# A sixteen-pair software pipeline on one core: the rounding number moves from VectorE to ScalarE, and every engine's loop gets another order

## What is computed

```python
x = _layernorm(x + _L0_attn_ref(x, ...))            # 512 -> 64 channels, 4 layers of decaying scan + MLP, -> 512
x = _layernorm(x + _L0_xattn_ref(x, ctx, ctx))      # autocorrelation attention
x = _layernorm(x + _L0_ffn_ref(x, weight, bias))    # x and weight rounded to MXFP4, one 512x512 product
```

## Time and profile before

| | us |
|---|---|
| median of 3 runs | 321.08 (320.82 to 321.69) |
| profiled execution, its own time | 323.65 |
| its span (first to last instruction) | 321.6 |
| first stage, span 0 to about 126 | 126 |
| pair loop, `attended(0)` to the end | 195 |
| one iteration in the middle of the loop | 9.95 |

### The profile page before, as it was taken

The page is one execution under the profiler, slowest core; times in us unless marked ns, Lnnn a source line. Parts: engine busy times, 40 slices in busy tenths (PEclk is TensorE's granted clock), DMA queues, the critical chain, the costliest instruction groups (busy, mean ns, idle before and its releaser), DMA issues.

```text
span 321.6 us, 4437 instructions
## 1 busy us (share of the span) xinstructions
PE 274.6 (85%) x1060; PEld 109.8 (34%) x1060; DVE 269.8 (84%) x871; ACT 231.1 (72%) x541; POOL 174.7 (54%) x226
## 2 busy tenths in 40 slices
PE   1597988989889887888998999999998888977762
PEld 1223222322222222254433554434444244422220
DVE  5969989889888894358999999999999989869580
ACT  6046789899799797967666687778877776745534
POOL 1026513204204014023378888999999999997842
PEclk9999899999999999999999999999999999979987
DMA  6999999602113200600000000111101102011122
GB/s 207 396 273 354 325 160 213 128 23 65 36 33 85 78 0 17 116 1 2 2 0 16 17 14 6 50 49 18 51 34 51 51 16 51 34 50 49 51 82 99
DMA packets 22576, 26.54 MB, mean 83 GB/s; under 512 B 10771, under 2 KB 11411, under 8 KB 22550
## 3 DMA queue, kind: packets, MB, share of 16 engines
q1 hardware_dynamic: 20470, 22.06, 21.9%
q0 software_dynamic: 2080, 4.19, 7.7%
HBM read 15.89 MB, written 4.19 MB: 62 GB/s over the span
## 4 chain that ended last, share of the span: by engine, by line
DVE 30%; ACT 20%; PE 18%; issue 15%; POOL 11%; DMA 3%; SPq 1%; POOLq 0%; DVEq 0%; ACTq 0%
DVE big L1172 5%; DVE m L1153 4%; DVE X L1107 3%; DVE big L1142 3%; DMA big<-in_xT_dram 3%; PE ps L380 3%; ACT big L654 3%; DVE ps L1203 3%; ACT L752 2%; DVE ps L1081 2%; ACT X L682 2%; PE ps L562 2%; POOL big L925 2%; POOL big L931 2%; DVE big L1277 2%
## 5 line engine op out<-in xcount | busy, mean ns | idle before, releaser
L654 ACT ACTIVATE big<-X,lnv 128x512 f32<-128x512 f32 x48 | 34.2, 713 | 15.0 <-DVE X L1107 15.0
L1107 DVE SCALAR_TENSOR_TENSOR X<-ps,X 128x512 f32<-128x512 f32 x48 | 32.1, 682 | 10.7 <-PE ps L415 6.1
L391 PE MATMUL ps<-ctx_ring,consts 64*128 64x512 f32 (+1 forms) x96 | 35.8, 643 | 0.0
L441 PEld LDWEIGHTS ps<-consts,big 96*128 96x128 f32 x256 | 29.8, 191 | 13.4 <-issue 10.6
L441 PE MATMUL ps<-consts,big 96*128 96x64 f32 x256 | 32.0, 278 | 1.1 <-DVE big L1142 1.1
L1184 DVE TENSOR_TENSOR big<-ps,ctxf 128x512 f32<-128x512 f32 x48 | 30.8, 683 | 2.0 <-PE ps L475 1.3
L682 ACT ACTIVATE X<-X,lnv 128x512 f32<-128x512 f32 x32 | 25.8, 808 | 0.6
L1172 DVE MATCH_REPLACE8 big<-w,big 128x64 f32<-128x64 f32 x128 | 25.1, 210 | 0.0
L838 POOL TENSOR_TENSOR big<-big 128x512 f32<-128x512 f32 x4 | 5.8, 1444 | 35.5 <-DVE big L1250 25.5
L918 POOL TENSOR_TENSOR big<-big 128x512 f32<-128x512 f32 x15 | 19.0, 1268 | 6.2 <-DVE big L1172 6.0
L1142 DVE TENSOR_TENSOR big<-ps,ctxf 96x512 f32<-96x512 f32 x32 | 20.4, 677 | 0.8 <-PE ps L428 0.8
(11 more groups left out here) (188 smaller groups left out, 675.9 us busy)
## 6 DMA issues: line engine op xcount, KB each, us to landing
big<-in_xT_dram SPq DMA_DIRECT2D x4, 1024.0 KB, 9.4
ctx_ring<-in_ctx_dram SPq DMA_DIRECT2D x16, 256.0 KB, 4.0
out_dram<-X SPq DMA_DIRECT2D x16, 256.0 KB, 2.0
X<-in_x_dram SPq DMA_DIRECT2D x2, 1536.0 KB, 11.4
X<-rows_sb POOLq DMA_DIRECT2D x1, 3072.0 KB, 21.6
X<-in_wq_dram SPq DMA_DIRECT2D x1, 1024.0 KB, 5.6
X<-in_x_dram SPq DMA_DIRECT2D x2, 512.0 KB, 3.9
X<-rows_sb POOLq DMA_DIRECT2D x1, 1024.0 KB, 8.0
```

What stands on the lines that cost most here:

```text
L391: mm(bank(LANE_BANK[lane]), mat((CY_0, CY_1, CY_C)[f])[half, :], ctx_ring[half, r * N:(r + 1) * N], start=True, stop=True).then_inc(s_cfor ...
L441: last = mm(ps[:, 2 * N + j * P + b * L:2 * N + j * P + (b + 1) * L], PQ[0:EVEN, b * N + j * P:b * N + (j + 1) * P], mat(IC_E)[0:EVEN, 0:L ...
L654: squared[k, n] = chain(a(JUNK[k], row(n), ACT.Square, bias=st[:, 0:1], scale=-float(V), accum_out=st[:, 2:3]))
L1107: stt(row(m), bank(b), 0.0, row(m), ALU.add, ALU.add, accum_out=st[:, 0:1]).then_inc(s_sum[k], 1)
```

## The change

On VectorE `rounding` becomes `exponents`: the mask alone. The number is made by a new ScalarE step `rounding_numbers`, one ACTIVATE (Copy) with scale and bias from bank 1 into `MB`: `SLOPE * e + FLOOR` lies in the same power of two as `max(e, 0.25) * MAGIC` for each e that can occur, so that it rounds alike. A semaphore `s_expo` passes from VectorE to ScalarE and to GpSimd's clamp. The loops of all five engines get another order and other distances; some one-time work (the last weight transposes, now into bank 7, and the last layernorm of the first stage) moves with them. `kept_busy` now stands at two places with 10 and 12 products; before 24 at six.

```diff
-DRAIN_BUSY = ((0, 4), (6, 6), (5, 3))
+DRAIN_BUSY = {LAST + 6: 10, LAST + 7: 12}
+SLOPE, FLOOR = 3.25 * 2.0 ** 20, 1.125 * 2.0 ** 20
...
             # sync
-            for n in range(PAIRS + 3):
+            for n in range(PAIRS + 5):
                 quantized_to_channels(n)
-                stored(n - 3)
+                stored(n - 5)
...
             # tensor
-            for t in range(1, PAIRS + 11):
-                weights_to_time(t - 7)
-                out_even(t - 8)
-                weight_rest_forms(t - 7)
-                weight_forms(t - 7)
-                correlation(t - 5)
...
-                query_forms(t - 4)
-                feed_forward(t - 10)
...
-                quantized_to_channels(t - 9)
-                out_rest(t - 7)
-                projection(t)
+            for t in range(1, PAIRS + 9):
+                weight_rest_forms(t - 5)
...
+                weight_forms(t - 5)
+                correlation(t - 3)
...
+                projection(t)
+                quantized_to_channels(t - 8)
+                feed_forward(t - 8)
+                query_forms(t - 2)
+                if t in DRAIN_BUSY:
+                    pe.wait_ge(s_sum[0], PAIRS)
+                    kept_busy(DRAIN_BUSY[t])
+                out_rest(t - 5)
+                weights_to_time(t - 4)
+                out_even(t - 5)
...
             # scalar
+            def rounding_numbers(n):
+                if here(n) and n < LAST:
+                    act.wait_ge(s_expo, n + 1)
+                    a(MB, bank(1), ACT.Copy, bias=FLOOR, scale=SLOPE).then_inc(s_magic[1], 1)
...
             # gpsimd, clamped
+                    pool.wait_ge(s_expo, n + 1)
+                    chain.then_wait(g_.tensor_scalar(VB, VB, 1.5, -1.5, ALU.min, ALU.max))
                     pool.wait_ge(s_magic[1], n + 1)
-                    chain.then_wait(g_.tensor_scalar(VB, VB, 1.5, -1.5, ALU.min, ALU.max))
...
             # vector
-                    do(ts(bank(1).bitcast(I32), VB.bitcast(I32), 0x7F800000, None, ALU.bitwise_and))
-                    ts(MB, bank(1), 0.25, MAGIC, ALU.max, ALU.mult).then_inc(s_magic[1], 1)
+                    ts(bank(1).bitcast(I32), VB.bitcast(I32), 0x7F800000, None, ALU.bitwise_and).then_inc(s_expo, 1)
```

More of the change, by code:

```diff
@@ L463, in weight_rest_forms @@
                     if n == 0:
-                        pe.wait_ge(s_act, 4 * SLOTS)
+                        pe.wait_ge(s_qe[0], VC)
                     if n >= 1:
@@ L602, in _ @@
                 slot(m)
[L603 to L618 removed]
+            for t in range(1, PAIRS + 9):
+                weight_rest_forms(t - 5)
+                if t == 4:
                     pe.wait_ge(s_sq1, SLOTS + 2)
                     mm(bank(4), mat(MEAN), SQ_LAST, start=True, stop=True).then_inc(s_var1, 1)
[L621 to L625 removed]
+                weight_forms(t - 5)
+                correlation(t - 3)
                 if t == 2:
                     mixed(SLOTS)
+                    transposes(0, VC, bank(7), XQ[0])
+                projection(t)
[8 more added lines that the diff above has]
+                out_even(t - 5)
         @block.scalar
@@ L779, in _ @@
             for t in range(PAIRS + 10):
-                squares(0, t)
-                corr_out(t - 3)
+                log_sum(t - 3)
+                squares(2, t - 9)
+                weights_out(t - 4)
+                rounding_numbers(t - 6)
                 if t == 3:
-                    weight_channels(VC - 1)
-                squares(2, t - 9)
-                if t == 2:
-                    act.wait_ge(s_mlp, SLOTS)
-                    a(SQ_LAST, XC[1], ACT.Square, bias=base[:, DEPTH:DEPTH + 1]).then_inc(s_sq1, 1)
-                quantized_out(t - 7)
-                factors(0, t - 1)
-                top_exponentials(t - 3)
-                weights_out(t - 4)
-                log_sum(t - 3)
-                normalise(0, t - 1)
-                last_factors(t - 9)
-                squares(1, t - 5)
-                factors(1, t - 5)
-                normalise(1, t - 5)
-                if t == 4:
                     act.wait_ge(s_var1, SLOTS + 2)
@@ L802, in _ @@
                 probabilities(t - 3)
+                squares(1, t - 5)
+                factors(1, t - 5)
+                normalise(1, t - 5)
+                squares(0, t)
+                corr_out(t - 2)
+                factors(0, t)
+                normalise(0, t)
+                top_exponentials(t - 2)
+                last_factors(t - 9)
+                if t == 0:
+                    act.wait_ge(s_mlp, SLOTS)
+                    a(SQ_LAST, XC[1], ACT.Square, bias=base[:, DEPTH:DEPTH + 1]).then_inc(s_sq1, 1)
+                if t == 1:
+                    weight_channels(VC - 1)
+                quantized_out(t - 8)
         @block.gpsimd
@@ L950, in block_scaled @@
                     scaled(1, row(n), n % 2, n + 1)
-            for t in range(PAIRS + 8):
-                block_scaled(t - 3)
+            for t in range(PAIRS + 9):
+                finished(t - 9)
+                rounded_off(t - 4, clamped(t - 4))
                 chosen(t - 1)
                 top_differences(t)
-                finished(t - 7)
-                mark = clamped(t - 3)
+                block_scaled(t - 3)
                 differences(t)
-                rounded_off(t - 3, mark)
         @block.vector
@@ L1193, in block_scales, with exponents @@
                     scales(1, row(n), n % 2, bank(4)[:, 0:NBLK])
-            def rounding(n):
+            def exponents(n):
                 if here(n) and n < LAST:
@@ L1285, in _ @@
                 slot(m)
-            for t in range(PAIRS + 9):
+            for t in range(PAIRS + 7):
+                top_sum(t - 3)
                 attended(t)
-                weight_products(t - 6)
-                block_scales(t - 7)
-                without_largest(t - 5)
-                last_chosen(t - 5)
-                fed(t - 9)
-                last_quantized(t - 7)
-                largest(t - 4)
-                if t == 6:
+                exponents(t - 6)
+                last_quantized(t - 6)
+                query_products(t - 2)
+                crossed(t - 5)
+                without_largest(t - 3)
+                last_chosen(t - 3)
+                weight_products(t - 4)
+                block_scales(t - 5)
+                largest(t - 2)
+                if t == 5:
                     last_norm(1, RS_LAST)
-                rounding(t - 7)
-                top_sum(t - 4)
-                query_products(t - 3)
-                crossed(t - 6)
+                fed(t - 7)
 def kernel(**inputs):
```

16 lines of the change are left out of this document (3 added, 13 removed).

## The result

| | before | changed |
|---|---|---|
| median | 322.27 (20 runs, 320.49 to 324.73) | **324.25** (20 runs, 322.67 to 330.71) |
| ratio, 95% interval | | **1.0059** (1.003 to 1.0087) |
| mean granted clock of an execution | 0.973 to 0.996 (runs of before beside the experiments) | 0.960 to 0.976 (one 0.949) |

The account below looks back on a forecast made before the run. It took a ring through ScalarE's layernorm and VectorE, closed once per 9.95 iteration, as the bound; GpSimd's 9.66 came next. Pairs 3 to 15 -4.0 and drain -1.0 gave -5.0: 316.1, range 312.5 to 320.4.

Parts of the forecast that it names:

- The middle: Pairs 3 to 15 by top_sum: 119.2 before, 115.2 after, from two iterations of 9.3 and ten of 9.66; -4.0.
- two places of 0.2: In TensorE's 9.79 iteration, L475 and L441 start later than the column stream needs; so 9.4 at least, 9.6 taken.
- the first window: One pair-loop iteration before the change, 232.03 to 241.98; attended was said to have run out ten iterations later.
- the hand-off: From MAX8's end through GpSimd and ScalarE to top_sum's start: 0.78, read from pair 0.
- VectorE's ring: VectorE's iteration, head to MAX8's end 8.41, plus hand-offs of 0.78 through GpSimd and ScalarE to top_sum: 9.2 together.
- its wait at the head: At the head of VectorE's iteration: a wait of some 0.5 for ScalarE's L699, a sign the forecast is right.
- The slower rival: ScalarE's waits stay and it becomes the bound: 10.3 an iteration, 324.3 in all; chance 0.12.
- The rival that TensorE holds: The iteration stays 9.95 because TensorE's 9.79 is real; only the drain gains: 320.1; chance 0.11.
- I leave pair 3 at 165.49: Ramp: pair 0 comes about 0.7 earlier, ScalarE's waiting order gives it back by pair 3; bounds -0.9 and +0.9.
- The drain: From top_sum to fed of pair 15: 31.1 before, 30.1 after; -1.0, bounds -2.5 and +1.2.
- The sum: Whole kernel: -4.0 for pairs 3 to 15 and -1.0 at the end make -5.0; span 316.6, forecast 316.1.
- the sign to look for: Sign of a wrong forecast: over 32 from last top_sum to last residual sum, TensorE's granted clock falling earlier than before.

Follow-up runs that it names:

- again: The changed kernel run and profiled once more, nothing altered: 325.6 (7 runs), ratio 1.0077 against the kernel before.
- warm: Changed kernel plus 16 idle TensorE products in the ramp's waits (iterations 2 and 4): 324.18 (12 runs), ratio 1.0004.
- drain_sbuf: Changed kernel with the block maxima of the last three pairs alone in SBUF, not bank 4: 322.91 (12 runs), ratio 1.0001.
- scales_sbuf: Changed kernel with the block maxima of the pairs in SBUF, not bank 4: 324.7 (12 runs), ratio 1.0075.
- no_holes: Changed kernel with drain_sbuf's edit, warm's idle products, 6 more in iteration 3, 14 behind the last out_even, 5 for 12 before the last transposes: 321.2, ratio 0.9978.

## Why the prediction was wrong

- **The middle**, pairs 3 to 15, forecast -4.0: measured -4.3. The mean iteration was right, its reason was not. I made GpSimd the bound at 9.66 and gave TensorE 9.6; TensorE's own round is 9.78, GpSimd's 9.49. The step that failed is the sentence on "two places of 0.2" inside TensorE's 9.79, which I took to be slack for the new order. They are no slack: from L467 to L475 and to L441 it takes 1.06 and 1.08 in before, and from L468 to L476 and to L442 1.06 and 1.06 in again (rows below). What the new neighbours cost (L487 to L456 takes 0.97 where L486 to L415 took 0.86, and L527 to L429 0.97 where L526 to L486 took 0.87), others gave back (L442 to L416 takes 1.83 where L441 to L428 took 1.92). That the total fits is luck: the twelve iterations aren't alike, four of 9.08 to 9.68 come first, then five of 9.78, then 9.64 and two of 9.47, 9.58 on average against the forecast's 9.60. Timelines of TensorE, before and again:

```profile
235.35 1.12 PE L467 MATMUL ps<-big,consts 128*128 128x512 f32 x2
236.41 1.15 PE L475 MATMUL ps<-big,consts 64*128 64x512 f32 x4
237.49 2.00 PE L441 MATMUL ps<-consts,big 96*128 96x64 f32 x16
```
```profile
238.52 1.13 PE L468 MATMUL ps<-big,consts 128*128 128x512 f32 x2
239.58 1.13 PE L476 MATMUL ps<-big,consts 64*128 64x512 f32 x4
240.64 2.00 PE L442 MATMUL ps<-consts,big 96*128 96x64 f32 x16
```

- **Smaller misreadings.** `attended` has run out two iterations after the first window, not ten. For pair 0 MAX8 ends at 140.87 (139.76 + 1.11), not 140.79, so the hand-off is 0.70 and VectorE's ring 9.1. Neither moves the sum.
- **VectorE and ScalarE.** VectorE is busy 9.23 of an iteration (forecast 9.02), and its wait at the head, 0.21, is for TensorE's L527 and not 0.5 for L699. The copy L684 takes 0.59 (forecast 0.60), and GpSimd waited for it 0.19 once in the middle. The slower rival, ScalarE's waits surviving, didn't come: ScalarE is busy 8.67 of 9.77. That its time, 324.3, is almost the measured 324.25 is chance: the iteration is not 10.3, and the loss lies at the ends. The rival that TensorE holds was right on the engine and wrong on the time.
- **The ramp**, "I leave pair 3 at 165.49": +2.8 from the first `attended`. This step failed. I followed who normalises first, and never asked what TensorE does between the last slot and the pair loop when its work comes earlier than its inputs. 2.4 of it goes with the clock (warm), 0.4 with the order itself.
- **The drain**, forecast -1.0, bound +1.2: +3.3. This step failed too. The sum followed GpSimd's and VectorE's chain of the last roundings and had no line for bank 4: `out_rest` of the last pair waits for `block_scales` of the pair before, which the new order puts behind `last_chosen` and the weight products. It is 2.75 (drain_sbuf, scales_sbuf). Without it the drain is still 0.5 over before and 1.5 over my sum. Of the 1.5, 0.7 lie between the last two `fed`, where the sum has 3.0 for transposes, copy and product and drain_sbuf 3.72: ScalarE's copy of the tile stands behind the third layernorm's factors of pair 14, and TensorE waits 1.51 for it. Another 0.5 is `last_quantized`, 5.49 for 5.0; GpSimd runs four `finished` beside it, where before has two. Both are read from traces and no run moves either; the last 0.3 is open. I had named the sign to look for, a drain above 32 with the clock falling earlier, but priced only `kept_busy`.
- **The sum**: -5.0 forecast; +2.1 between the traces, +2.0 between the medians (ratio 1.0059). With the wait for bank 4 gone the ratio is 1.000, with both ends mended 0.998, and not the forecast's 0.985. The 1.3% that is left is in part in the ends, 0.8 us in no_holes' ramp and 1.6 in its drain over my sum. In part it is the yardstick: my sum stood on a trace of before at clock 0.978, whose own time, 323.65, is 1.4 above the median of 20. (The time outside the span explains nothing of that; in all runs of before on record it is 1.8 to 2.3.) How the rest divides stays open.

## What to carry to other kernels

A shorter iteration is worth its length times the pairs only if the ramp and the drain are walked through with the same care, buffer by buffer: in a software pipeline a change of order moves every release as well. When several engines are full, take a little away from each in turn to see which one sets the iteration; the chain of waits can't say it. And here the small part of the change, one instruction to another engine, brought 0.5 to 0.8% alone and the whole of the shorter iteration in the middle (9.79). The new order around it gained 2.65 us between pairs 3 and 15 over that and lost 3.2 in the ramp and 2.3 in the drain.
